# A graph layer with attention, a linear-attention branch and gated experts: the first stage's loads, norm roots and walk in another order

## The reference

```python
xn = layernorm(x)                     # (x - mean) / sqrt(var + 1e-5)
q, k, v = xn @ Wq.T + bq, xn @ Wk.T + bk, xn @ Wv.T + bv      # 8 heads of 32
e = edge_attr @ We.T
alpha = sum over c of q[dst] * (k[src] + e) / sqrt(32)
w = softmax of alpha over the edges with the same dst
gnn = segment_sum((v[src] + e) * w, dst) + xn @ Wskip.T + bskip
mix = linear attention over all nodes, projection, norm, 256-1024-256 block, norm
x1 = x + gnn + mix
out = x1 + sum over 8 experts of gate * expert(layernorm(x1))      # 3 products each, softmax gate
```

## Time and profile before

| | us |
|---|---|
| median of 3 runs | 3412.22 (3410.17 to 3415.22) |
| the profiled execution | 3411.48, its span 3409.4 |
| PE busy | 3125.4 (92%) |
| DVE busy | 2794.6 (82%) |
| ACT, POOL busy | 1692.1, 1670.1 |

### The profile page before, as it was taken

How to read it: one execution, slowest core, us unless ns; L and a number is a source line. 1 busy time by engine, 2 the same in 40 slices (tenths; PEclk the granted TensorE clock), 3 DMA queues, 4 the chain that set the end, 5 groups by cost and what they waited for, 6 DMA issues and landing times.

```text
span 3409.4 us, 71878 instructions
## 1 busy us (share of the span) xinstructions
PE 3125.4 (92%) x17162; PEld 2443.6 (72%) x17162; DVE 2794.6 (82%) x5782; ACT 1692.1 (50%) x4461; POOL 1670.1 (49%) x1834
## 2 busy tenths in 40 slices
PE   4997999999999999999999488888889999999999
PEld 3776566666666666666666355555579999999999
DVE  6776789888889898888888989989977677776775
ACT  1222334334444343443443356655567777777776
POOL 2222777777777777777777278877710000000000
PEclk9998899999999999999999699999989999999999
DMA  7344999999999999999999377777710000000000
GB/s 185 116 123 140 248 265 268 260 261 265 265 267 267 265 268 263 265 266 264 260 266 261 102 231 224 227 228 226 229 37 15 12 18 12 12 18 12 17 14 9
DMA packets 521332, 592.15 MB, mean 174 GB/s; under 512 B 188089, under 2 KB 397272, under 8 KB 520996
## 3 DMA queue, kind: packets, MB, share of 16 engines
q1 hardware_dynamic: 310638, 347.54, 34.9%
q0 software_dynamic: 202016, 232.77, 26.0%
q10 hardware_dynamic: 8473, 9.56, 0.9%
HBM read 425.33 MB, written 163.37 MB: 173 GB/s over the span
## 4 chain that ended last, share of the span: by engine, by line
PE 49%; DMA 17%; DVE 15%; issue 7%; SPq 5%; POOL 3%; DVEq 3%; ACT 1%; ACTq 0%; POOLq 0%
PE psum L750 10%; PE psum L752 10%; PE psum L751 10%; PE psum L968 8%; DMA weights<-kv_tab,idx 6%; DMA ve_d<-weights 5%; DVE weights L1515 3%; PE psum L812 3%; PE psum L828 2%; DMA region_r<-kv_tab,idx 2%; POOL weights L660 2%; DVE part L1529 2%; DVEq L1709 2%; DVE region_s L1706 1%; DVE kv_more L1515 1%
## 5 line engine op out<-in xcount | busy, mean ns | idle before, releaser
L660 POOL DMA_INDIRECT weights<-kv_tab,idx x450 | 551.9, 1226 | 244.8 <-issue 157.4
L828 PE MATMUL psum<-region_x,weights 125*125 x1800 | 487.2, 394 | 70.1 <-DVE weights L1523 23.4
L968 PE MATMUL psum<-region_s 125*125 125x264 f32 x1800 | 453.5, 401 | 71.6 <-DVE region_s L1706 69.3
L1272 ACT ACTIVATE region_s<-psum,bns 128x250 f32<-128x250 f32 x800 | 402.7, 554 | 229.9 <-PE psum L752 229.9
L812 PE MATMUL psum<-we,weights 64*125 64x256 f32 x1800 | 512.9, 406 | 0.0
L1759 DVE TENSOR_TENSOR parts_h<-region_s,parts_h 128x500 fp32r<-128x500 f32 x400 | 270.6, 682 | 241.4 <-ACT parts_h L1276 207.8
L968 PEld LDWEIGHTS psum<-region_s 125*125 125x125 f32 x1800 | 305.3, 188 | 219.7 <-DVE region_x L1695 64.5
L1142 ACT ACTIVATE weights<-psum,region_s 125x250 f32<-125x250 f32 x450 | 211.1, 469 | 504.3 <-PE psum L820 503.5
L828 PEld LDWEIGHTS psum<-region_x,weights 125*125 125x125 f32 x1800 | 321.9, 190 | 174.2 <-issue 135.2
L812 PEld LDWEIGHTS psum<-we,weights 64*125 64x125 f32 x1800 | 299.0, 185 | 180.7 <-issue 151.8
L660 POOL DMA_INDIRECT kv_more<-kv_tab,idx x300 | 370.5, 1235 | 93.5 <-issue 77.2
(11 more groups left out here) (260 smaller groups left out, 7586.2 us busy)
## 6 DMA issues: line engine op xcount, KB each, us to landing
region_s<-ve_d SPq DMA_DIRECT2D x450, 256.0 KB, 3.0
ve_d<-weights SPq DMA_DIRECT2D x225, 256.0 KB
ve_d<-kv_more SPq DMA_DIRECT2D x150, 256.0 KB
weights<-in_attr_t SPq DMA_DIRECT2D x450, 62.5 KB
ve_d<-region_r SPq DMA_DIRECT2D x75, 256.0 KB
kv_tab<-region_s SPq DMA_DIRECT2D x50, 224.0 KB
region_s<-ab_d SPq DMA_DIRECT2D x450, 1.0 KB
weights<-kv_tab,idx POOLq DMA_INDIRECT x450
```

The costliest lines, as they stand in the source:

```text
L660: nc.gpsimd.indirect_dma_start(kg[r][0:T, w, :], None, kv_tab, bass.IndirectOffsetOnAxis(idx[:, r, w:w + 1], 0)).then_inc(gathered[r], 16)
L828: last = mm(psum[0:T, 2 + s % 2, w * D:(w + 1) * D], hott[:, s % RA, w * T:(w + 1) * T], q_all[:, bass.ds(j, 1), :].rearrange("p o d -> p ...
L968: last = mm(bank, hot[:, s, w, :], pv[:, s, w, 0:PV], start=(w == 0), stop=(w == 1))
L1272: last = fn(fh[:, layer, o, :], psum[:, bk + e % 2, o * BN:(o + 1) * BN], ACT.Relu, bias=bns[:, layer, 1, col:col + 1], scale=bns[:, layer ...
```

## The change

The first stage is rearranged in six ways.

1. SP issues the x blocks 1 to 4 only when the constants and the two weight tables have landed, and then the four small constants of stage two. POOL waits for the same before its seven small loads.
2. The roots are made by POOL with a power operation: ten tiles at the start, then two tiles at a time behind every pair of tiles, up to pair 19. DVE's `ln` waits for `x_root`.
3. DVE's code for tiles 0 to 39 is unrolled. The walk is cut into 27 pieces, one behind each of the tiles 10 to 36. `scores` is cleared at the start, `coef` and `ab_b` in the pieces 25 and 26, `jneg` is made in front of tile 40.
4. SP moves the walk through memory behind the stores of tile 35.
5. The branch's weights and `pick` are loaded behind the first attribute load of stage two (`c_mix`); PE waits for them in front of the first branch product.
6. `pick` (the chunk table) lies in another buffer.

SP:

```diff
+            sp.wait_ge(c_a, CONST_A)
+            sp.wait_ge(c_w, CONST_W)
             for i in range(1, NT // XC):
                 load_x(i)
+            sp.dma_start(we[:, :], a["w_e"]).then_inc(c_b, 16)
...
-            twice(sp, NT, store_a)
+            store_a(0, 0)
+            store_a(1, 1)
+            for first, end in ((1, 18), (18, NT // 2)):
+                with sp.Fori(first, end) as it:
+                    store_a(it * 2, 0)
+                    store_a(it * 2 + 1, 1)
+                if first == 1:
+                    move_walk()
...
+            def load_branch():
+                sp.dma_start(wmq, a["w_mq"].rearrange("(c p) n -> p c n", p=128)).then_inc(c_mix, 16)
...
+                    if k == 0:
+                        load_branch()
```

POOL:

```diff
+            pool.wait_ge(c_a, CONST_A)
+            pool.wait_ge(c_w, CONST_W)
...
+            def x_roots(t, n):
+                part_x = xstat[:, bass.ds(t, n), :]
+                order(nc.gpsimd.tensor_tensor(part_x[:, :, 3], part_x[:, :, 1], epsilons[:, 0:n], ALU.add))
+                nc.gpsimd.tensor_tensor(part_x[:, :, 2], part_x[:, :, 3], halves[:, 0:n], ALU.pow).then_inc(x_root, 1)
+            pool.wait_ge(x_stat, XC)
+            x_roots(0, XC)
...
-            twice(pool, NT, a_body)
+            def a_pair(t, more):
+                a_body(t, 0)
+                a_body(t + 1, 1)
+                if more:
+                    pool.wait_ge(x_stat, t + XC + 2)
+                    pool.sem_inc(gather_go, 1)
+                    x_roots(t + XC, 2)
+                    order.reset()
```

PE:

```diff
+                        if b == 0:
+                            pe.wait_ge(c_mix, CONST_MIX)
```

DVE:

```diff
+            def walk_piece(n):
+                if n == 0:
+                    dve.wait_ge(dst_c_in, 128)
+                    dve.wait_ge(walk_steps, 4)
+                    nc.vector.tensor_copy(node[:, :], node_i[:, :])
+                    order(tt(wf, wz, wi, ALU.add))
+                elif 1 <= n <= SU:
+                    if n == 1:
+                        order(nc.vector.tensor_copy(walk_s[:, 0, :], walk_k[:, 0:SU]))
+                    order(ts(wl, wf, walk_s[:, 0, n - 1:n], 0.0, ALU.is_lt, ALU.add, accum_out=walk_s[:, 1, n - 1:n]))
...
             def ln(t, u, roots=1):
                 wait(dve, xn_turned, t - 1)
                 wait(dve, xnb_ready, t - 1)
+                if not (isinstance(t, int) and t < XC):
+                    dve.wait_ge(x_root, roots)
...
-            def x_roots(i):
-                dve.wait_ge(x_stat, (i + 1) * XC)
-                part_x = xstat[:, i * XC:(i + 1) * XC, :]
-                rsqrt(part_x[:, :, 1:2], LN_EPS, part_x[:, :, 2:3], part_x[:, :, 3:4])
...
+            def a_pair(pair, stats_ahead, last_pair=False):
                 for u in range(2):
+                    a_body(pair * 2 + u, u, pair, last_tile=last_pair and u == 1)
                     if stats_ahead:
+                        x_stats(pair * 2 + u + XC, u)
+                    if isinstance(pair, int) and pair >= XC // 2:
+                        walk_piece(pair * 2 + u - XC)
                 order.reset()
```

More of the change, by code:

```diff
@@ L223, in build @@
         xsix = weights[0:T, 12014 + 4 * NT:12014 + 4 * NT + 60].rearrange("p (t k) -> p t k", t=10)
+        x_consts = weights[0:T, 12014 + 4 * NT + 24:12014 + 4 * NT + 44].rearrange("p (k t) -> p k t", k=2)
         xn = carve(0, 2, D, parts=T)
@@ L338, in build @@
         turned, turned_out = sem("turned"), sem("turned_out")
-        mask_in, mask_ready = [sem(f"mask_in{i}") for i in range(3)], sem("mask_ready")
+        mask_in = [sem(f"mask_in{i}") for i in range(3)]
+        x_root = sem("x_root")
         ends_moved, carried = sem("ends_moved"), sem("carried")
@@ L442, in _ @@
-            with nc.allow_non_contiguous_dma(reason="one row to every partition"):
-                sp.dma_start(jb_all, jb_d.rearrange("i s -> (i s)").partition_broadcast(T)).then_inc(walk_in, 16)
+            sp.dma_start(we[:, :], a["w_e"]).then_inc(c_b, 16)
+            sp.dma_start(iota[:, :], a["iota"]).then_inc(c_b, 16)
+            sp.dma_start(wr[:, :, :], a["w_r"].rearrange("(c p) n -> p c n", p=128)).then_inc(c_b, 16)
+            sp.dma_start(bo_e[:, :], a["bo_e"]).then_inc(c_b, 16)
@@ new lines, in move_walk @@
+            def move_walk():
+                sp.wait_ge(walk_ready, 1)
+                sp.dma_start(walk_d.rearrange("w (i s) -> i w s", s=SU), walk_i[:, :, :]).then_inc(walk_out, 16)
+                sp.dma_start(jb_d, walk_s[:, 3, :]).then_inc(walk_out, 16)
+                sp.wait_ge(ab_ready, 1)
+                sp.dma_start(ab_d.rearrange("h (p n) -> p h n", p=T), dst_ab).then_inc(ab_out, 16)
+                sp.wait_ge(ab_ready, 2)
+                sp.dma_start(mask_d.rearrange("(p n) -> p n", p=T), mask_c).then_inc(ab_out, 16)
+                sp.wait_ge(setup_ready, WALK_CLEAR)
+                sp.wait_ge(walk_out, 32)
+                sp.dma_start(walk[0:1, 0, 0:STEPS], walk_d[0:1, :]).then_inc(walk_in, 16)
+                sp.dma_start(walk[0:1, 1, LAGQ:LAGQ + STEPS], walk_d[1:2, :]).then_inc(walk_in, 16)
+                sp.dma_start(walk[0:1, 2, LAGP:LAGP + STEPS], walk_d[2:3, :]).then_inc(walk_in, 16)
+                with nc.allow_non_contiguous_dma(reason="one row to every partition"):
+                    sp.dma_start(jb_all, jb_d.rearrange("i s -> (i s)").partition_broadcast(T)).then_inc(walk_in, 16)
@@ L1361, in _ @@
             nc.vector.memset(vone.rearrange("p u c n -> p (u c n)"), 1.0).then_inc(setup_ready, 1)
-            dve.wait_ge(dst_c_in, 96)
-            dve.wait_ge(walk_steps, 4)
-            nc.vector.tensor_copy(node[:, :], node_i[:, :])
-            order(tt(wf, wz, wi, ALU.add))
-            order(nc.vector.tensor_copy(walk_s[:, 0, :], walk_k[:, 0:SU]))
-            for s in range(SU):
-                order(ts(wl, wf, walk_s[:, 0, s:s + 1], 0.0, ALU.is_lt, ALU.add, accum_out=walk_s[:, 1, s:s + 1]))
@@ L1378, in _ @@
-            order(nc.vector.tensor_copy(walk_i[:, 1, :], walk_s[:, 4, :]))
-            order(nc.vector.memset(walk_s[:, 5, :], 0.0))
-            for c in range(1, CH):
-                order(stt(walk_s[:, 5, :], walk_s[:, 1, :], float(CT // 2 * c), walk_s[:, 5, :], ALU.is_ge, ALU.add))
-            order(ts(walk_s[:, 4, :], walk_s[:, 1, :], float(2 * CH), None, ALU.mult))
-            order(stt(walk_s[:, 4, :], walk_s[:, 5, :], float(1 - CT * CH), walk_s[:, 4, :], ALU.mult, ALU.add))
-            nc.vector.tensor_copy(walk_i[:, 2, :], walk_s[:, 4, :]).then_inc(walk_ready, 1)
```

183 lines of the change are left out of this document (97 added, 86 removed).

## The result

| | kernel before | changed kernel |
|---|---|---|
| median of 11 runs each, same chip | 3414.85 us (3410.17 to 3420.67) | 3427.17 us (3420.61 to 3441.74) |
| profiled execution, its span | 3411.48, 3409.4 | 3424.73, 3422.9 |

The ratio is 1.004, with a 95% interval of 1.0026 to 1.0053: slower by 0.4%. The forecast was 3418 with a range of 3385 to 3440.

The account below looks back on a forecast made before the run. PE was taken to bound the kernel, busy for 92% of the span. From the profiled 3411.5 us, terms of -19, +30, 0, -4 and -1 gave 3417.5; with 0.7 for the median of runs 3418, range 3385 to 3440.

Parts of the forecast that it names:

- Part 2: Stage one, roots on POOL: its wait delays the next tile's additions, DVE and PE, 1.6 us a pair, 19 pairs, +30.
- The four block ends of before: Stage one: PE's idle while DVE makes ten roots, and three clock falls, go away; 19.2 us, so -19.
- The front's -4: Start of stage one: tile 2 begins at 56 us instead of 60, bounds -8 and +1.
- part 3: Stage one, the walk in 27 pieces on DVE: 0, since PE's products cover them; 4 us if cover falls short.
- At most +2: Behind tile 35: the cost in us of the walk's four stores and four loads between two SP loops.
- part 5: Step from stage one to stage two: constants early, branch weights late; -1 us, bounds -5 and +4.
- they take 10 us: 341: Step to stage two: 2.6 MB of branch weights at 265 GB/s land at 341 us, releasing PE's first branch product.
- The forecast's 331: Step to stage two: time in us when SP issues the branch weights, behind the first attribute load.
- the next ones about 2 earlier: Start of stage two: edge sums after the first come about 2 us earlier, their gathers having landed by then.
- nothing in the change touches those: Stages behind the first: a change of more than 5 us in any would show the prediction wrong.
- the right case: The likeliest case, 57%: POOL's wait reaches PE in every second tile of stage one; 3418 us, span 3403 to 3432.
- the one to which it gave 0.40: Whole kernel: the chance that the change measures slower, above 3419 us; faster had 0.32, same 0.28.

Follow-up runs that it names:

- the run with the loads at once: Changed kernel without the waits that make SP hold x blocks 1 to 4 for constants and weight tables; ratio 1.0019 to the kernel before.
- The version that beats both: Changed kernel with roots a pair later, walk's moves spread, branch tables early, first branch product waiting for `wmq` alone; 0.9916, again 0.9905 of the kernel before.
- the three edits: Changed kernel with roots a pair later, walk's moves spread and branch tables early; ratio 0.9926 to the kernel before, median 3387.35 us.

## Why the prediction was right, and where it was wrong

**Right: the mechanism and its price.** Part 2 named the instruction that waits, what is queued behind it and who waits for that. Of its steps, with M = 136.89, the start of that tile's `state` group: the statistics end at M+1.84 (forecast M+1.92), POOL's last addition at M+4.68 (M+4.67), L1494 starts at M+4.77 (M+4.95), and PE's product at M+6.63 (M+6.86). The idle is 1.17 to 1.26 us in steady state, 1.44 in the first three pairs, 1.32 and 1.62 once each, and the tile is late by 1.45 (forecast 1.6). Over the stage, from the gaps between `state` groups: 18 tiles take 27.7 us more than 4.85 each, and the nineteenth 1.5, together 29 against the forecast +30. The four block ends of before are worth 19.2 by the same count, as forecast (-19). Tile 2 came at 56.40 (forecast 56). Leaving these gaps out is worth 25 us in the experiment, where the walk's moves take 3 of them back.

**Right in sum, with terms that were off both ways.** The front's -4 had put 3 us of later x loads and 3.5 for four constants against the walk's 11 us of SP time. The x loads ended at 42.24, not 45, and 1.7 behind those of the run with the loads at once; the four constants took 5.5, and tile 0's last store 5.5 to land instead of 4 to 4.6. That these cancel, and tile 2 came at 56.40, is luck.

**Wrong, part 3: the walk's moves.** "At most +2" was given because POOL, ACT and DVE wait for those stores only two tiles later. The moves cost PE 6 us (a tile of 12.34 us where 4.85 would be and 1.45 belong to the pair). The two tiles of cover were counted against 3.5 us of issue time; left out was that the store behind eight more DMAs is itself blocked for 2.98, and that the clock falls as well (0.66 from 262 to 272 us, around the idle of 5.40).

**Wrong, part 5: the step, -1 forecast, +10.1 measured** (26.1 to 36.2 us from the last `state` group to the first edge sum). The step that failed is "they take 10 us: 341". The start of the loads was right. The forecast's 331 is in the time of the kernel before, 11.5 us behind its last `state` group; the tables are issued from 340.38 on, 10.8 behind that of the changed kernel, after the state, three reads of the walk into registers (1.48, 1.72 and 1.34 us) and the step's own loads. But from that first issue to the last landing, at 357.95, it is 17.6 us. The two windows above say why: 220 and 182 GB/s over 10 us each are 4.0 MB, and the tables are only 2.6 of them. The mask and the block of `xnt_d` had been issued just before (at 334.9 to 335.4), and the first gathers run beside them. So the bytes of the others were left out, and the 265 GB/s were not reached. The first sum comes 7.8 us behind the landing (forecast 7.6), and thus 7 too late. The other 4 us of the miss are "the next ones about 2 earlier": nothing is given back, the first and the last edge sum are late by the same 20 us. Issuing the tables early gave back 11 of 11.8 in the experiment, so the order of these loads is what the step cost.

**Wrong: "nothing in the change touches those".** The sums by node are 7.8 us shorter. The form of DVE's code in the first stage is enough for it in one trace (513.4), and is not the whole cause, which stays open. The prediction called more than 5 us in a later stage a sign against it, and that sign came.

The sum, then: stage one +10.1 where the terms give -3.7 - 19.2 + 29.2 + 6.0 = 12.3 (2.2 less, since most tiles of before took some hundredths more than 4.85), the step +10.1, later stages about -7, together 13.5. The forecast's terms gave +6: it missed 17 us of cost (6 and 11) and 9 of gain. It chose the right case, and its median of 3418 lies 9 us below the measured 3427.17. That this is inside the range is in part luck: misses of both signs met. The outcome, slower by more than 7 us, is the one to which it gave 0.40.

**The version that beats both** keeps what was good in the change (no roots on DVE, no walk in the front) and mends the three places: 0.9916 and 0.9905 of the kernel before on two chips, 29 to 32 us less. Against the changed kernel (1.004 and 1.0046) it is 42 to 48 us. It is not told apart from the one that has only the three edits.

## What to carry to other kernels

When work moves to an idle engine, don't ask whether that engine has time but what is queued behind the new wait; here waiting for statistics two tiles older took 25 us off with the same instructions. Loads and stores that are moved as a bunch cost where they land: spread them, and for a table that an early product needs, count all the bytes that are in flight with it, not its own alone. A stage that "isn't touched" should still be looked at, with a repeat of both kernels, before a difference is explained.

## What the runs showed of the hardware

- The granted clock of TensorE stayed at 1.00 through gaps of 1.17 to 1.62 us every 11.1 us, and averaged 0.88 to 0.90 with gaps of 1.9 to 2.4 us about every 13.4. So 0.7 us more of a wait cost 2.3 us a pair. The gap's length alone does not decide: three gaps of 1.93 to 2.46 us there, and one of 3.44 in the kernel before (at 153.50), were not followed by a fall. The Trainium skill (TensorE: Matmul & The Clock Gate, on the HAM clock gate) says that activity lifts the clock from a throttled default; the two runs agree with it in sign: the clock fell to 1.2 GHz behind idle time and rose again with work.
- A power on POOL takes 0.71 us for 125x2 elements and 2.00 for the first ten columns; behind it the addition that it needs takes 0.19, with 0.18 between the two.
- The same DVE operation of 125x512 elements has a mean of 685 to 701 ns, and a POOL operation of 125x125 one of 873 to 946, by the kernel in which they run, at equal work.
